# Both layer norms of a Mamba and mixture-of-experts block: the sums for mean and variance taken by ScalarE instead of VectorE

## The reference, cut to what matters

```
def _layernorm(x, axis=-1, eps=1e-05):
    m = jnp.mean(x, axis=axis, keepdims=True)
    v = jnp.var(x, axis=axis, keepdims=True)
    return (x - m) / jnp.sqrt(v + eps)

x = hidden_states                # (8, 512, 512): 4096 tokens of 512
x = x + mamba(_layernorm(x))     # in_proj 512 -> 2 x 1024, causal conv of 4 taps, silu, x_proj, dt_proj,
                                 # softplus, selective scan over 512 tokens with 16 states a channel,
                                 # D skip, gate silu(z), out_proj 1024 -> 512
x = x + experts(_layernorm(x))   # 8 experts, top 2 of a softmax, 512 -> 1792 -> 512, silu gate
```

## Time and profile before

| | |
|---|---|
| median of 3 runs | 4304.62 us (4304.53 to 4308.6) |
| profiled execution, its own time | 4304.38 us |
| its span | 4302.6 us |
| busy, share of the span | TensorE 91%, VectorE 84%, GpSimd 60%, ScalarE 47% |
| chain that ended last | TensorE 41% of the span, all of it in the expert stage, from 2442 us on |
| mean granted TensorE clock | 0.957 |

### The profile page before, as it was taken

How to read it: one execution, slowest core, us unless ns; L and a number is a source line. 1 busy time by engine, 2 the same in 40 slices (tenths; PEclk the granted TensorE clock), 3 DMA queues, 4 the chain that set the end, 5 groups by cost and what they waited for, 6 DMA issues and landing times. The chain is left out here.

```text
span 4302.6 us, 72404 instructions
## 1 busy us (share of the span) xinstructions
PE 3894.7 (91%) x25436; PEld 3380.4 (79%) x25436; DVE 3594.8 (84%) x5245; ACT 2043.5 (47%) x4314; POOL 2569.3 (60%) x2169
## 2 busy tenths in 40 slices
PE   6687889889988988898888599999999999999898
PEld 5565677677767776777676499999999999999886
DVE  5999998999999999999999588878878888788500
ACT  7677777777877778777766111111111111111100
POOL 3677778777876787687777244544545545445300
PEclk9888899999999999999998699999999999999999
DMA  4112353554445354535443555555555665655495
GB/s 162 64 40 93 119 174 114 172 165 151 142 157 174 116 167 162 174 111 177 162 150 101 176 187 176 192 182 181 185 176 181 195 184 177 190 176 190 136 331 192
DMA packets 422581, 694.11 MB, mean 161 GB/s; under 512 B 19680, under 2 KB 209760, under 8 KB 414048
## 3 DMA queue, kind: packets, MB, share of 16 engines
q1 hardware_dynamic: 406160, 655.24, 45.8%
q0 software_dynamic: 14768, 34.41, 4.2%
q10 hardware_dynamic: 1440, 1.81, 0.1%
HBM read 668.25 MB, written 45.95 MB: 166 GB/s over the span
## 5 line engine op out<-in xcount | busy, mean ns | idle before, releaser
L635 POOL TENSOR_TENSOR hs<-hs,bc 128x1024 f32<-128x1024 f32 x512 | 1214.5, 2372 | 307.6 <-DVE hs L1347 285.5
L1347 DVE TENSOR_TENSOR_SCAN hs<-dA,pU 128x1024 f32<-128x1024 f32 x512 | 1168.5, 2282 | 44.5 <-ACT dA L754 22.2
L754 ACT ACTIVATE dA<-delta,aneg 128x255 f32<-128x255 f32 x2048 | 852.1, 517 | 36.9 <-DVE hs L1347 33.7
L1146 PE MATMUL pY<-ident,hs 128*128 128x128 f32 x4096 | 566.1, 286 | 237.3 <-POOL hs L635 237.2
L1146 PEld LDWEIGHTS pY<-ident,hs 128*128 128x128 f32 x4096 | 488.4, 147 | 344.7 <-POOL hs L635 167.4
L1330 DVE TENSOR_TENSOR pU<-pZ,bc 128x1024 f32<-128x1024 f32 x512 | 629.7, 1230 | 30.5 <-issue 0.5
L1821 POOL TENSOR_TENSOR hsum<-hT 128x128 f32<-128x128 f32 x168 | 152.9, 910 | 585.1 <-DVE hT L2169 585.1
L1030 PE MATMUL pM<-xnT,win 128*128 128x256 f32 x1680 | 409.7, 400 | 30.9 <-DMA win<-in_w_in 25.1
L1030 PEld LDWEIGHTS pM<-xnT,win 128*128 128x128 f32 x1680 | 331.7, 203 | 80.8 <-issue 28.3
L2033 PE MATMUL ps<-xT,w1s 128*128 128x128 f32 x2688 | 357.8, 276 | 7.3 <-POOL xt L1837 5.3
L2033 PE MATMUL ps<-xt,su 128*128 128x128 f32 x2688 | 357.2, 276 | 0.0
(11 more groups left out here) (347 smaller groups left out, 7374.5 us busy)
## 6 DMA issues: line engine op xcount, KB each, us to landing
ew<-in_w SPq DMA_DIRECT2D x273, 512.0 KB, 4.1
w1s<-in_w SPq DMA_DIRECT2D x96, 1024.0 KB
w3s<-in_w SPq DMA_DIRECT2D x96, 1024.0 KB
w2s<-in_w SPq DMA_DIRECT2D x96, 1024.0 KB
win<-in_w_in SPq DMA_DIRECT2D x128, 512.0 KB, 4.7
bc<-bc_d SPq DMA_DIRECT2D x64, 1024.0 KB, 9.1
w1s<-in_w SPq DMA_DIRECT2D x32, 512.0 KB
w3s<-in_w SPq DMA_DIRECT2D x32, 512.0 KB
```

What stands on the lines that cost most here:

```text
L635: pool.tensor_tensor(hs[b][:, :, :], hs[b][:, :, :], bc[:, N + g * PN:N + (g + 1) * PN, :], ALU.mult)\
L754: e = act.activation(dA[k % NB][:, i, 1:T], delta[:, c, 1:T], ACT.Exp, scale=aneg[:, c, n:n + 1])
L1146: m = pe.matmul(pY[c % 2][:, t * P:(t + 1) * P], hs[k % NB][:, i, t * P:(t + 1) * P], ident[:, :], start=g == 0 and i == 0 and t == 0, sto ...
L1347: dve.tensor_tensor_scan(hs[b][:, :, :].rearrange("p n t -> p (n t)"), dA[b][:, :, :].rearrange("p n t -> p (n t)"), pU[:, :, :].rearrange ...
```

## The change

Mean and variance come from ScalarE. For each tile of 128x512, `mean_of` passes the rows through Identity with scale -1/512, and the accumulator output writes minus the mean; `squares_of` passes them through Square with that as bias, and the accumulator output writes the sum of the squared deviations. The full-size output of both goes to a tile that nobody reads at the time (`waste`, in `xnT`). `root` takes the square root of sum/512 + eps. VectorE keeps one tiny instruction for the variance plus eps (`variance`), the Newton step and the scales.

Second norm, in steps that also scan: mean and squares of tile 0 stand in ScalarE's slot 7, ahead of the silu; mean and squares of tile 1, and the root, in slot 8. VectorE takes the root at (8, 1), as before. First norm, from the rows of step 2 on: all four passes and the root stand in ScalarE's slot 14, behind `copy_z`; VectorE takes the root at (15, 1) in place of (15, 0). The first norm of the rows of steps 0 and 1, and the second norm in the drain (step 16), are made as before.

```diff
+            def mean_of(rows, t, mv, to, step):
+                return act.activation(to, rows[:, t, 0:D], ACT.Identity, scale=-1.0 / D, accum_out=mv[:, t, 0:1]).then_inc(step, 1)
+            def squares_of(rows, t, mv, to, step):
+                return act.activation(to, rows[:, t, 0:D], ACT.Square, bias=mv[:, t, 0:1], accum_out=mv[:, t, 1:2]).then_inc(step, 1)
+            def root(mv, sdev, ready):
+                act.activation(sdev[:, :], mv[:, :, 1], ACT.Sqrt, bias=series[:, 2:3], scale=1.0 / D).then_inc(ready, 1)
...
+                waste = [xnT[odd][:, 2 * t:2 * t + 2, :].rearrange("p d q -> p (d q)") for t in range(TT)]
...
-                    if u == 7 and back:
-                        ge(act, var2, r + 1)
+                    if u == 7 and back and scan:
+                        ge(act, x1_ready, TT * r + 1)
+                        ge(act, scale2, r)
+                        mean_of(rows_of(r), 0, mv2, waste[0], moment2)
+                        ge(act, moment2, 2 * TT * r + 1)
+                        squares_of(rows_of(r), 0, mv2, waste[1], moment2)
+                    if u == 8 and back and scan:
+                        ge(act, x1_ready, TT * r + 2)
+                        ge(act, moment2, 2 * TT * r + 2)
+                        mean_of(rows_of(r), 1, mv2, waste[0], moment2)
+                        ge(act, moment2, 2 * TT * r + 3)
+                        squares_of(rows_of(r), 1, mv2, waste[1], moment2)
+                        ge(act, moment2, 2 * TT * r + 4)
+                        root(mv2, tiny2[1], sd2)
+                    if u == 7 and back and not scan:
+                        ge(act, var2, 1)
                         act.activation(tiny2[1][:, :], mv2[:, :, 1], ACT.Sqrt, bias=series[:, 2:3]).then_inc(sd2, 1)
...
-                    if u == 13 and ln1:
-                        ge(act, var1, s + 3)
-                        act.activation(tiny1[1][:, :], mv1[:, :, 1], ACT.Sqrt, bias=series[:, 2:3]).then_inc(sd1, 1)
                     if 12 <= u <= 15 and front:
                         copy_z(u - 12, f, szf)
+                    if u == SLOTS - 2 and ln1:
+                        ge(act, logits_mm, r + 1)
+                        ge(act, xf_in, 16 * s + 48)
+                        for t in range(TT):
+                            mean_of(xf, t, mv1, waste[t], moment1)
+                        ge(act, moment1, 2 * TT * s + TT)
+                        for t in range(TT):
+                            squares_of(xf, t, mv1, waste[t], moment1)
+                        ge(act, moment1, 2 * TT * s + 2 * TT)
+                        root(mv1, tiny1[1], sd1)
...
+            def variance(ch, mv, tiny):
+                ch.done(dve.tensor_scalar(tiny[0][:, :], mv[:, :, 1], 1.0 / D, EPS, ALU.mult, ALU.add))
...
+            def ln1_next(n, i):
+                if i == 0:
+                    ln1_chain[0] = Chain(ln1_step, 2 * LN1S_FIRST + LN1S * (n - 2))
+                    dve.wait_ge(sd1, n + 1)
+                ch = ln1_chain[0]
+                if i < 4:
+                    newton(ch, tiny1, i)
+                if i == 0:
+                    variance(ch, mv1, tiny1)
+                if i == 4:
+                    scales(ch, mv1, tiny1, 0, scale1)
...
-                        if at == (5, 0):
+                        if at == (5, 0) and not scan:
                             stats2(0)
...
-                        if at == (7, 0):
+                        if at == (7, 0) and not scan:
                             stats2(1)
-                        if at == (7, 1):
+                        if at == (7, 1) and not scan:
                             aggregate(bk, st2, mv2)
-                        if at == (7, 2):
+                        if at == (7, 2) and not scan:
                             bk.settle()
                             dve.tensor_scalar(tiny2[0][:, :], mv2[:, :, 1], EPS, None, ALU.add).then_inc(var2, 1)
                         if at == (8, 1):
                             ge(dve, sd2, r + 1)
                         if u == 8 and g >= 1:
                             newton(bk, tiny2, g - 1)
+                        if at == (8, 1) and scan:
+                            variance(bk, mv2, tiny2)
...
                     if ln1_too:
-                        if at in ((12, 2), (12, 3), (13, 1), (13, 2)):
-                            ln1(s + 2, ((12, 2), (12, 3), (13, 1), (13, 2)).index(at))
-                        if u == 15:
-                            ln1(s + 2, 4 + g)
+                        if u == 15 and g >= 1:
+                            ln1_next(s + 2, g - 1)
```

More of the change, by code:

```diff
@@ L233, in mixer @@
         sd1 = sem("sd1")
+        moment1 = sem("moment1")
+        moment2 = sem("moment2")
         xn1 = sem("xn1")
@@ L322, in mixer @@
         NSET = 15 + NB
-        LN1S, BACKS, SPS, LNS = 8, 36, 4, 5
+        LN1S_FIRST, LN1S, BACKS, BACKS_LAST, SPS, LNS = 8, 6, 34, 36, 4, 5
         CONVS = (5 * PAIRS, 4 * PAIRS)
@@ L1260, in aggregate, with scales @@
                 ch.done(i)
-            def scales(ch, mv, tiny, n, ready):
+            def scales(ch, mv, tiny, n, ready, sign=1.0):
                 ch.settle()
                 ch.done(dve.tensor_copy(rs[n][:, :], tiny[4][:, :]))
-                dve.scalar_tensor_tensor(nb[n][:, :], tiny[4][:, :], -1.0, mv[:, :, 0], ALU.mult, ALU.mult)\
+                dve.scalar_tensor_tensor(nb[n][:, :], tiny[4][:, :], sign, mv[:, :, 0], ALU.mult, ALU.mult)\
                    .then_inc(ready, 1)
+            def variance(ch, mv, tiny):
+                ch.done(dve.tensor_scalar(tiny[0][:, :], mv[:, :, 1], 1.0 / D, EPS, ALU.mult, ALU.add))
             ln1_chain = [None]
             LN1_PARTS = 9
+            def ln1_next(n, i):
[9 more added lines that the diff above has]
+                    scales(ch, mv1, tiny1, 0, scale1)
+                    assert ch.n == LN1S
             def ln1(n, i):
                 if i == 0:
-                    ln1_chain[0] = Chain(ln1_step, LN1S * n)
+                    ln1_chain[0] = Chain(ln1_step, LN1S_FIRST * n)
                 ch = ln1_chain[0]
@@ L1289, in ln1 @@
                 if i == 8:
-                    scales(ch, mv1, tiny1, 0, scale1)
-                    assert ch.n == LN1S
+                    scales(ch, mv1, tiny1, 0, scale1, -1.0)
+                    assert ch.n == LN1S_FIRST
             def step(s, odd):
@@ L1446, in place @@
                         dve.tensor_scalar(tok[:, :], tok[:, :], float(T), None, ALU.add).then_inc(rows_ready, 1)
-                        assert bk.n == BACKS, bk.n
+                        assert bk.n == (BACKS if scan else BACKS_LAST), bk.n
                 def pick(i):
@@ L1537, in beside @@
                         if at == (9, 1):
-                            scales(bk, mv2, tiny2, 1, scale2)
+                            scales(bk, mv2, tiny2, 1, scale2, 1.0 if scan else -1.0)
                         if at == (12, 2):
@@ L1585, in step @@
                 if ln1_too:
-                    ln1(s + 2, 8)
+                    ln1_next(s + 2, 3)
                 if picks:
-                    for i in range(4):
+                    pick(0)
+                if ln1_too:
+                    ln1_next(s + 2, 4)
+                if picks:
+                    for i in range(1, 4):
                         pick(i)
@@ L1661, in link @@
                 dve.wait_ge(plan, count[0])
-            dve.wait_ge(back_step, BACKS * STEPS)
+            dve.wait_ge(back_step, BACKS * (STEPS - 1) + BACKS_LAST)
             dve.wait_ge(e_step, E_STEPS * EARLY)
```

## The result

The changed kernel takes 4426.84 us (4424.3 to 4427.65, 4 runs), the kernel before 4305.8 in the same comparison: ratio 1.0281, 95% interval 1.0266 to 1.0295. The forecast was 4429. The profiled execution has a span of 4425.9 us, 123.3 more than before, all of it in the mixer.

What follows compares the result with a forecast made beforehand. VectorE's queue was taken to bound the mixer. Two waits for roots, with TensorE held between them, net of regained waits, gave 11 x 10.0 us plus smaller steps, 125 us on 4304: 4429 us, range 4350 to 4475.

Steps and rivals of the forecast that it cites:

- Sum and size: Whole mixer: steps 3 to 13 each 10.0 us longer, 110 us, with the other steps together 125 us.
- The rest: Mixer steps outside 3 to 13: step 14 7.5 us, steps 1 and 2 6, steps 0 and 15 0.5 and 1.
- First wait: VectorE in slot 8 waits for the second norm's root, 12.7 us in even steps, 7.5 in odd.
- swallowed: Slot 8: 1.4 us of statistics saved ahead of the root gain nothing, ScalarE's time there hanging on TensorE and GpSimd.
- Second wait: VectorE at slot 15 waits for the first norm's root: 4.9 us in step 8, mean 3.9 over steps 3 to 13.
- What TensorE adds: TensorE, from slot 8: held 6.1 us by piece 17, plus 0.7 for the clock, carried on to slot 14.
- The premise: Mixer steps 1 to 14: VectorE's queue sets the time, so a microsecond taken off it is one gained.
- rival 1: Slots 7 and 8: the root is in time, waits are hidden, VectorE keeps its 41 us: 4263 us; chance 4%.
- Half of it (3): TensorE catches up by hidden slack and the second root is in time: 59 us or less, 4314 to 4370; 17%.
- More (5): Clock falls and long accumulator writes pile up over the whole step: above 4470 us; chance 12%.
- Signs named beforehand: New profile: VectorE busy about 40 us less, ScalarE 90 to 100 more, TensorE waiting some 5 us for GpSimd in slot 8.

Runs made afterwards that it cites:

- e4: Changed kernel with, in slot 8 alone, VectorE's gating product moved ahead of its wait for the root; 4411.84 us, ratio 1.0251 to the kernel before.
- e7: Changed kernel with the second norm's passes in slots 6 and 7, the first norm's passes and root in slot 13; 4301.1 us, ratio 0.9997 to before.
- e3: Kernel before plus the added ScalarE passes at the changed kernel's places, sums unread, roots and VectorE's statistics kept; 4306.29 us, ratio 1.0010.

## Why the prediction was right, and where it was not

**Sum and size.** From VectorE's arrival at the root in step 3 (563.26 after, 559.72 before) to that in step 14 (2290.97 after, 2176.04 before) lie 11 steps; they grew by 111.4 us, 10.1 a step, where 10.0 were forecast. The rest, 12 us, was forecast as 15. That a step came out so close is in part luck. From ScalarE's copy of y in slot 8 to that in slot 14 a step grew by 7.6 us in the mean (54.3 to 61.9), where the forecast has 6.3 (its 6.8 less the 0.5 that it puts ahead of the copy). Over the rest of the step it grew by 2.6 in place of 3.7. The two misses cancel.

**First wait.** Forecast 12.7 and 7.5 us, measured 12.1 and 6.7. The pass with its accumulator was priced by the normalising pass, 800 ns, and up to 0.20 for the write. The trace has 0.63 for the mean, 0.72 for the squares, and 0.19 to 0.20 for each write: a pair takes 1.58 us and not 2.1. This term of the sum was sized too high, by 1.0 us for the two pairs. The other way, VectorE comes 0.46 us earlier against ScalarE's silu in step 8 than before (0.24 in step 9) and waits that much longer: of the 1.4 us of its statistics, which I called swallowed, a part was not. 12.7 less 1.0 plus 0.5 is the 12.1 measured, 7.5 less 1.0 plus 0.2 the 6.7.

**Second wait.** The root comes 4.48 us after its place (1416.27 to 1420.75 in step 8), forecast 5.3. VectorE waited 4.01 us in each of steps 3 to 13, where I wrote 4 to 5. It is the same in every step because the place no longer lies 0.4 to 2.8 us ahead of VectorE: VectorE itself is released by TensorE's ranks just before (1.90 us in step 8), and the ranks and the copy of y hang on the same TensorE.

```profile
1416.27 0.63 ACT L689 ACTIVATE xnT<-xf 128x512 f32<-128x512 f32 x1
...
1416.59 0.18 DVE L1489 TENSOR_TENSOR pZ<-pS,ebase 128x16 f32<-128x16 f32 x1 [1.90 <-PE pS L1159]
```

**What TensorE adds.** This is the step that was near in size and wrong in cause. I had piece 17 hold it by 6.1 us, plus 0.7 for the clock. It is held by the gating product, which I had only counted as 0.41 us of VectorE's queue and not looked up who waits for it. In step 8 piece 17 is summed 12.97 us behind ScalarE's copy of y where it was 5.33: 7.6 us more (7.3 in the mean of steps 3 to 13), where the forecast has 5.6 and 0.7 for the clock. Of these some 2.7 are the slow clock (1.97 for 1.04 and 5.53 for the 3.74 that the same group takes one slot before), more than the upper end that I gave. With the product out of the way (e4) my mechanism comes up in its place. That TensorE carries the hold to slot 14 is right: in the mean all of it arrives there, 7.6 us. In step 8 it is only 5.8 us, because a slow group, 5.38 us in the earlier trace rows, ran in 3.69 behind the same transfer in this trace. Over steps 3 to 14 this group is slow 5 times of 12 before and 6 times of 12 after.

**The premise.** "A microsecond taken off VectorE is one gained" was wrong. It did no harm, because the change put waits of 166 us into VectorE's queue, but it was the reason for the 4263 us of rival 1. e7 is that rival made true, with roots nearly in time, and it takes 4301: 36 us less work for VectorE, 33 us more waiting. What I had before me and read past is that TensorE in step 8 has no idle from slot 8 to slot 14 but 0.84 us and 2.46 us for a transfer, the same fact that I used for the hold. That this is what holds VectorE up is likely and not shown. By e7, rival 1 would have been level with the kernel before, and not faster.

**Rivals.** Half of it (3) needed TensorE to catch up, and it didn't: between slots 9 and 14 of step 8 it stands still for 0.85 and 2.31 us, before for 0.84 and 2.46. More (5) needed accumulator writes of 0.5 us, and they took 0.2. That the added work costs as such was no rival in the prediction; e3 excludes it.

**Signs named beforehand.** VectorE's busy time fell by 32.7 us over the span (forecast 40), ScalarE's rose by 86.1 (forecast 90 to 100), the expert stage kept its time. TensorE's wait in slot 8 is 4.5 to 5.3 us in steps 3 to 14 (forecast some 5), but for VectorE, not for GpSimd. The wait of VectorE for the ranks, 4.0 to 25.3 us, was missed.

**The page on table loads.** The Trainium skill, page "ScalarE: Activation LUTs", section "What ACT_TABLE_LOAD costs", would have the root 1.4 us later for a drain. In this trace the root starts at 1357.20, behind a load from 1355.91 of 1.28 us, and the next load at 1357.52: no drain. The same section of the Trainium skill gives 186 ns + 0.833 ns an element for a pass with immediate operands and 93 ns more for a pointer. An estimate from these figures is 613 and 706 ns at 512 elements; the trace has 0.63 and 0.72 us. This would have been the better price for the passes than the row that I took. For the accumulator write the Trainium skill, page "VectorE: DVE Perf Modes" (section "Two Vector instructions with no wait between them") states for VectorE that such an operation is two instructions; here the same is seen on ScalarE, at 0.19 to 0.20 us.

## What to carry to other kernels

Here work moved to an engine with a quarter of its time free was paid by the place in its queue, not by its length: the same passes cost a thousandth with their result unused, 122 us where another engine waits for them, and nothing one slot earlier. Ask for each result what stands ahead of it in the new queue, and what stands behind the waiting instruction in the old one, including small products that a third engine needs. And before counting the busy time that is removed as gain, look whether another engine runs without gaps beside the first; then the time removed may turn into waiting, as 33 of 36 us did in e7.

## What the runs showed of the hardware

- An activation with accumulator output is followed by an instruction of its own, `ACTIVATION_READ_ACCUMULATOR`, 186 to 201 ns in the mean. Two such passes in a row start 0.61 us apart (1416.27 and 1416.88 for the means of step 8), so that the read overlaps the next pass.
- TensorE at rest for 4.51 us (step 8 of the changed kernel) came back at a granted clock of 0.50 over the next 5 us, where it had 1.00 from 1350.0 to 1354.7 us ahead of the stop. Its groups took 1.5 and 1.9 times as long. The cost was 2.7 us, and 2.4 us behind the stop of 4.25 us in e4. Shorter stops for a transfer were followed by a slow group in some steps (5.38 us for 3.62) and by none in others (3.69 us). In steps 3 to 14 of the kernel before, the slow ones came 5 times of 12, behind stops of 1.98 to 2.46 us, the others behind stops of 1.88 to 2.40 us. One of the others, in the changed kernel:

```profile
1410.90 3.69 PE L1068 MATMUL pM<-xnT,win 128*128 128x256 f32 x16 [2.31 <-DMA win<-in_w_in]
```

The length of the stop doesn't tell the two apart. What decides was not tried.
